# First and second layers of finished node tiles, placed by a table of trips instead of from trip 14 on

## The reference, cut to what matters

```python
# dst = sorted (6250 * u ** 2), u uniform; N_VERTEX rows are those of x
aggr = segment_sum(edge_attr, dst, num_segments=6250)          # 100,000 x 256 -> 6250 x 256
collected = concatenate([layernorm(x), aggr], axis=-1)         # 6250 x 512
h = relu(collected @ W1 + b1)                                  # first layer, 512 -> 256
h = relu(h @ W2 + b2)                                          # second layer
x = x + h @ W3 + b3                                            # third layer
x = x + ffn(layernorm(x))       # slice attention over all nodes, 8 heads of 64, then W_out
```

## Time and profile before

| | us |
|---|---|
| median of 3 runs (lowest, highest) | 680.67 (680.16, 681.75) |
| the profiled execution's own time | 680.57 |
| its span, first to last instruction | 678.8 |
| TensorE busy in the span | 603.0 (89%) |
| VectorE / ScalarE / GpSimd busy | 400.4 / 286.8 / 242.9 |
| moved by DMA | 133.88 MB, mean 197 GB/s |
| last turn of the edge part (L1243) starts | 324.17 |

### The profile page before, as it was taken

The page is one execution under the profiler, slowest core; times in us unless marked ns, Lnnn a source line. Parts: engine busy times, 40 slices in busy tenths (PEclk is TensorE's granted clock), DMA queues, the critical chain, the costliest instruction groups (busy, mean ns, idle before and its releaser), DMA issues.

```text
span 678.8 us, 12657 instructions
## 1 busy us (share of the span) xinstructions
PE 603.0 (89%) x3481; PEld 363.8 (54%) x3481; DVE 400.4 (59%) x1104; ACT 286.8 (42%) x422; POOL 242.9 (36%) x322
## 2 busy tenths in 40 slices
PE   5677777878798999899999889999999999799997
PEld 2355555545443444344689634444444443688886
DVE  6644444456454454444468888888888888522222
ACT  4244444545223223222210045555545454677773
POOL 3244444435000000000032366666666666344441
PEclk9799999989999999999999899999999999999999
DMA  8999999999999989994110123434343434122221
GB/s 305 339 403 406 405 403 407 392 385 383 386 378 328 329 289 321 314 323 148 31 43 3 32 47 62 77 62 77 62 77 62 76 63 77 16 78 77 77 77 69
DMA packets 107135, 133.88 MB, mean 197 GB/s; under 512 B 57595, under 2 KB 59601, under 8 KB 107109
## 3 DMA queue, kind: packets, MB, share of 16 engines
q1 hardware_dynamic: 106293, 133.29, 58.9%
q10 hardware_dynamic: 816, 0.26, 0.2%
HBM read 114.29 MB, written 6.40 MB: 178 GB/s over the span
## 4 chain that ended last, share of the span: by engine, by line
PE 59%; DMA 26%; DVE 7%; issue 4%; SPq 1%; DVEq 1%; POOL 1%; ACT 0%; POOLq 0%
DMA x_sb<-x_in 19%; PE ps L1520 12%; PE ps L1433 12%; PE ps L1450 11%; DMA ring_mem<-edge_attr_in 8%; PE ps L1249 6%; PE ps L1255 6%; PE ps L1212 4%; DVE big L933 2%; PE ps L1364 2%; PE ps L1426 2%; PE ps L1243 1%; DVE x_sb L1009 1%; DVE bn L1013 1%; DVEq L933 0%
## 5 line engine op out<-in xcount | busy, mean ns | idle before, releaser
L1212 PE MATMUL ps<-ring_mem,side 128*32 128x256 f32 (+1 forms) x1596 | 104.3, 395 | 44.6 <-DMA ring_mem<-edge_attr_in 44.6
L933 DVE TENSOR_TENSOR big<-big,ps 128x64 f32 x319 | 70.7, 222 | 109.5 <-PE ps L1243 72.1
L1212 PEld LDWEIGHTS ps<-ring_mem,side 128*32 128x32 f32 (+1 forms) x1596 | 51.0, 112 | 82.5 <-issue 46.1
L1433 PE MATMUL ps<-ring_mem,xn 128*128 128x512 f32 x196 | 93.3, 599 | 0.8 <-DVE ring_mem L1093 0.7
L1450 PE MATMUL ps<-side,ring_mem 128*128 128x512 f32 x196 | 92.3, 593 | 1.9 <-ACT ring_mem L740 1.9
L697 ACT ACTIVATE side<-ps 128x512 f32<-128x512 f32 (+1 forms) x50 | 25.6, 511 | 151.9 <-PE ps L1212 151.9
L629 POOL TENSOR_TENSOR ring_mem<-ring_mem 128x512 f32<-128x512 f32 x49 | 67.3, 1374 | 30.7 <-DVE ring_mem L1093 30.0
L1520 PE MATMUL ps<-side,ring_mem 128*128 128x256 f32 x360 | 77.9, 379 | 0.0
L1520 PEld LDWEIGHTS ps<-side,ring_mem 128*128 128x128 f32 x360 | 68.4, 190 | 9.3
L755 ACT ACTIVATE ring_mem<-ring_mem 128x512 f32<-128x512 f32 x49 | 30.9, 630 | 91.5 <-POOL ring_mem L622 91.5
L800 ACT ACTIVATE ring_mem<-big 128x1024 uint16 (+1 forms) x45 | 60.7, 1359 | 15.5 <-PE ps L1520 15.5
(11 more groups left out here) (136 smaller groups left out, 815.2 us busy)
## 6 DMA issues: line engine op xcount, KB each, us to landing
ring_mem<-edge_attr_in SPq DMA_DIRECT2D x84, 1024.0 KB, 8.5
ring_mem<-edge_attr_in SPq DMA_DIRECT2D x62, 256.0 KB, 4.3
x_sb<-x_in SPq DMA_DIRECT2D x24, 256.0 KB, 5.6
result<-ring_mem SPq DMA_DIRECT2D x24, 256.0 KB, 2.0
big<-side SPq DMA_TRANSPOSE x49, 3.0
side<-L_gnn_W_in SPq DMA_DIRECT2D x2, 256.0 KB, 10.1
ring_mem<-L_ffn_W_x_in SPq DMA_DIRECT2D x2, 256.0 KB, 2.8
ring_mem<-L_ffn_W_out_in SPq DMA_DIRECT2D x1, 512.0 KB, 3.9
```

The source lines that it names most:

```text
L933: dve.tensor_tensor(win, win, found[:, :, q * WINDOW:(q + 1) * WINDOW], ALU.add).then_inc(groups_added, 1)
L1212: return mm(ps[q * WINDOW:(q + 1) * WINDOW, SUM_BANKS[h], col:col + F], lhsT=hot[0:parts, h * 2 + j, t, :], rhs=ring8[0:parts, h * 2 + j, ...
L1433: last = mm(ps[:, 4 + k, :], lhsT=xn[:, r, k * P:(k + 1) * P], rhs=soft[:, r, :], start=isinstance(t, int) and t == 3, stop=isinstance(t, ...
```

## The change

The rule "first layer of tile i - 14, second of the tile before" becomes two tables of trips:

- the first layer's edge half runs in trips 10, 11, 13, 15, 16, 18, 19, 20, 22, 23, 24 (tiles 0 to 10), the second layer in trips 12, 14, 15, 17, 18, 20 to 24 (tiles 0 to 9). Where a trip has both, the second layer stands in front of the first, on TensorE, and `relu_two` in front of `relu_one` on ScalarE.
- in trips 10 to 13 they stand beside the work on x. `first_layer_x` writes both halves into bank 5 and counts once; the second layer uses banks 6 and 7 up to trip 13 and 4 and 5 after that.
- trips 10 to 24 are all written out; the loop over trips 2 to 9 stays.
- the weights of both layers are loaded in batch 3 instead of batch 26.
- the bounds `lowest` follow the table, by ten iotas on GpSimd instead of two.

```diff
@@ -43,9 +43,14 @@
 X_TRIPS = 13
-H1E_TRIP = 14
-H1E_TILES = 11
-H2_TILES = H1E_TILES - 1
+
+H1E_AT = {10: 0, 11: 1, 13: 2, 15: 3, 16: 4, 18: 5, 19: 6, 20: 7, 22: 8, 23: 9, 24: 10}
+H2_AT = {12: 0, 14: 1, 15: 2, 17: 3, 18: 4, 20: 5, 21: 6, 22: 7, 23: 8, 24: 9}
+H1E_TILES = len(H1E_AT)
+H2_TILES = len(H2_AT)
+TRIPS = 25
+
+H1E_RUNS = ((0, 10, 2), (2, 13, 1), (3, 15, 2), (5, 18, 3), (8, 22, 3))
 H2_CREDIT = 2
@@ -76,16 +81,8 @@
     trip(1, 2, P, "x")
     with eng.Fori(2, TWOS // UNROLL) as i:
         trip(i, 2, P, "x")
-    with eng.Fori(TWOS // UNROLL, X_TRIPS - 1) as i:
-        trip(i, 4, P, "x")
-    trip(X_TRIPS - 1, 4, P, "x")
-    trip(X_TRIPS, 4, P, "x")
-    trip(H1E_TRIP, 4, P, "h1")
-    with eng.Fori(H1E_TRIP + 1, FOURS // UNROLL) as i:
-        trip(i, 4, P, "h2")
-    with eng.Fori(FOURS // UNROLL, H1E_TRIP + H1E_TILES - 1) as i:
-        trip(i, 4, LAST_P, "h2")
-    trip(H1E_TRIP + H1E_TILES - 1, 4, LAST_P, "h2")
+    for i in range(TWOS // UNROLL, TRIPS):
+        trip(i, 4, P if i < FOURS // UNROLL else LAST_P, "x" if i <= X_TRIPS else "")
 def run_steps(eng, step, total, peel_front, loop_trips):
@@ -139,7 +136,7 @@
     assert F == KF * P and P == 2 * G and D == G and S == 512 and AGG >= N + WINDOW
     MLP_CHUNKS = (TILES - 1) // 4
     H1E_NODES = H1E_TILES * 4 * P
-    assert CHUNKS == UNROLL * (H1E_TRIP + H1E_TILES) and TAIL_GROUPS == 3 and (E - E_TAIL) % ROWS_PER_PART == 0
+    assert CHUNKS == UNROLL * TRIPS and TAIL_GROUPS == 3 and (E - E_TAIL) % ROWS_PER_PART == 0
     assert X_PAIRS == 2 * (X_TRIPS - 1) and H1E_TILES == MLP_CHUNKS - 1
     with ExitStack() as ctx:
@@ -368,6 +365,10 @@
         block = ctx.enter_context(nc.Block())
+        def h2_banks(i):
+
+            return [ps[:, (6 if i <= X_TRIPS else 4) + m, :] for m in range(KF)]
+
         def words(v):
             return v.bitcast(U16).rearrange("p (n h) -> p h n", h=2)
@@ -443,7 +444,7 @@
                     sp.dma_start(tiles_of(b * 2, 2).rearrange("p t f -> p (t f)"),
                                  x[bass.ds(b * (2 * P), 2 * P), :].rearrange("(p t) f -> p (t f)", p=P)
                                  ).then_inc(x_in, 16)
-                if isinstance(b, int) and b == X_PAIRS + 2:
+                if isinstance(b, int) and b == 3:
                     sp.dma_start(w1b_sb, w1[F:2 * F, :].rearrange("(k p) n -> p k n", p=P)).then_inc(w1b_in, 16)
                     sp.dma_start(w2_sb, w2.rearrange("(k p) n -> p k n", p=P)).then_inc(w2_in, 16)
@@ -552,8 +553,9 @@
             pool.wait_ge(rel_clear, 1)
             for a, first in enumerate((TWOS, FOURS)):
-                pool.iota(steps_of[:, a, :], [[UNROLL, H1E_TILES]], base=UNROLL * H1E_TRIP - first, channel_multiplier=-1,
-                          allow_small_or_imprecise_dtypes=True).then_inc(lowest_ready, 1)
+                for tile, at, n in H1E_RUNS:
+                    pool.iota(steps_of[:, a, tile:tile + n], [[UNROLL, n]], base=UNROLL * at - first, channel_multiplier=-1,
+                              allow_small_or_imprecise_dtypes=True).then_inc(lowest_ready, 1)
             pool.wait_ge(hot_ready, 1)
             pool.memset(big[:, CLEAR_A:KF * AGG], 0.0).then_inc(agg_clear, 1)
             pool.wait_ge(consts, 6)
@@ -673,9 +675,9 @@
                                ACT.Copy).then_inc(ln_t_ready, 1)
             def copy_h1x(i, n):
+                act.wait_ge(h1x_psum, i + 1)
                 for m in range(KF):
-                    act.wait_ge(h1x_psum, i * 2 + (m + 1))
-                    act.activation(h1x[:, m, bass.ds(i * 2 * P, n * P)], ps[:, 5 + m, 0:n * P],
+                    act.activation(h1x[:, m, bass.ds(i * 2 * P, n * P)], ps[:, 5, m * 2 * P:m * 2 * P + n * P],
                                    ACT.Identity, bias=b1_sb[:, m:m + 1]).then_inc(h1x_ready, 1)
             far_reg = []
@@ -704,10 +706,10 @@
                         norm_rows(b - 1, 2)
                     if isinstance(b, int) and b == X_PAIRS + 1:
                         norm_rows(X_PAIRS, 1)
-                elif h == 1:
-                    relu_one(i - H1E_TRIP, 4 * P)
-                    if what == "h2":
-                        relu_two(i - (H1E_TRIP + 1), 4 * P, [ps[:, 4 + m, :] for m in range(KF)])
+                if h == 1 and isinstance(i, int) and i in H2_AT:
+                    relu_two(H2_AT[i], 4 * P, h2_banks(i))
+                if h == 1 and isinstance(i, int) and i in H1E_AT:
+                    relu_one(H1E_AT[i], 4 * P)
                 if isinstance(b, int) and b == X_PAIRS + 3:
                     far_reg.append(act.value_load(far_i[0:1, 0:1], min_val=0, max_val=1))
@@ -852,10 +854,10 @@
             dve.tensor_scalar(row_ok[:, :], row_no[:, :], float(LAST_ROWS), None, ALU.is_lt).then_inc(groups_added, CREDIT)
             bases_one = into_bases(0, TWOS, 2, 7, 0)
-            dve.wait_ge(lowest_ready, 2)
+            dve.wait_ge(lowest_ready, 2 * len(H1E_RUNS))
             dve.tensor_scalar(steps_of, steps_of, 0.0, float(UNROLL * P), ALU.is_le, ALU.mult).then_inc(lowest_ready, 1)
             dve.memset(far_one[:, :], 0.0).then_inc(h2_ready, H2_CREDIT)
-            dve.wait_ge(lowest_ready, 3)
+            dve.wait_ge(lowest_ready, 2 * len(H1E_RUNS) + 1)
             dve.tensor_reduce(lowest[:, :], steps_of, AX.X, ALU.add).then_inc(h1e_added, 1)
             dve.wait_ge(h1e_added, 1)
             dve.wait_ge(dst_in, 16 * 5)
@@ -912,10 +914,9 @@
                     dve.wait_ge(win_psum, b * 2 + 2)
                     for j in range(2):
                         one_hot(b * 2 + (UNROLL + j), h * 2 + j)
-                if what != "x":
-                    if h == 0:
-                        dve.wait_ge(h1x_ready, 2 * (X_PAIRS + 1))
-                    add_h1e(i - H1E_TRIP, h)
+                if isinstance(i, int) and i in H1E_AT:
+                    dve.wait_ge(h1x_ready, 4 * (H1E_AT[i] + 1))
+                    add_h1e(H1E_AT[i], h)
                 if h == 0:
                     n_regs = UNROLL * groups
                     dve.load(base_regs[0:n_regs], base_i[0:1, bass.ds(sums_ahead(b * 2, groups), n_regs)])
@@ -1032,6 +1033,7 @@
                 folded[0] += 1
                 return folded[0]
+            dve.wait_ge(h1x_ready, 2 * (X_PAIRS + 1))
             for m in range(KF):
                 add_h1e(MLP_CHUNKS - 1, m)
             for m in range(KF):
@@ -1266,22 +1268,29 @@
                         first_layer_x(b - 3, 1 if isinstance(b, int) and b == X_PAIRS + 3 else 2)
                     if past(b, 2) and before(b, X_PAIRS + 3):
                         ln_transposes(b - 2, 1 if isinstance(b, int) and b == X_PAIRS + 2 else 2)
-                else:
-
+                if isinstance(i, int) and i in H2_AT:
+                    j = H2_AT[i]
+                    pe.wait_ge(w2_in, 16)
+                    pe.wait_ge(h1_ready, j + 1)
+                    if j == 0:
+                        pe.wait_ge(h1e_added, 2 * 2 + 1)
+                    elif j == 1:
+                        pe.wait_ge(h1x_ready, 2 * (X_PAIRS + 1))
+                    else:
+                        pe.wait_ge(h2_ready, H2_CREDIT + 2 * (j - 1) + h + 1)
+                    last = second_layer(j, h, h2_banks(i)[h], 4 * P)
+                    if h == KF - 1:
+                        last.then_inc(l2_psum, 1)
+                if isinstance(i, int) and i in H1E_AT:
+
+                    j = H1E_AT[i]
+                    pe.wait_ge(w1b_in, 16)
+                    pe.wait_ge(h1e_added, 2 * j + 1)
+                    if j == 2:
+                        pe.wait_ge(h2_ready, H2_CREDIT + 2)
                     if h == 0:
-                        pe.wait_ge(w1b_in, 16)
-                        pe.wait_ge(h1x_ready, 2 * (X_PAIRS + 1))
                         pe.wait_ge(groups_added, sums_ahead(b * 2, groups) + CREDIT)
-                    pe.wait_ge(h1e_added, (i - H1E_TRIP) * 2 + 1)
-                    first_layer_edges(i - H1E_TRIP, h).then_inc(h1e_psum, 1)
-                    if what == "h2":
-                        if h == 0:
-                            pe.wait_ge(w2_in, 16)
-                            pe.wait_ge(h1_ready, i - H1E_TRIP)
-                        pe.wait_ge(h2_ready, (i - H1E_TRIP) * 2 + (H2_CREDIT - 3 + h))
-                        last = second_layer(i - (H1E_TRIP + 1), h, ps[:, 4 + h, :], 4 * P)
-                        if h == KF - 1:
-                            last.then_inc(l2_psum, 1)
+                    first_layer_edges(j, h).then_inc(h1e_psum, 1)
                 turn(b, h, groups)
                 if isinstance(b, int) and b == 1:
                     rest_of_table()
@@ -1305,9 +1314,9 @@
                     pe.wait_ge(h1x_ready, i * 2)
                 for m in range(KF):
                     for k in range(KF):
-                        last = mm(ps[:, 5 + m, 0:n * P], lhsT=w1a_sb[:, k, m * P:(m + 1) * P],
+                        last = mm(ps[:, 5, m * 2 * P:m * 2 * P + n * P], lhsT=w1a_sb[:, k, m * P:(m + 1) * P],
```

(2 more changed lines are left out.)

## The result

The changed kernel takes 664.5 us in the median of four runs (661.8 to 665.7), the kernel before beside it 681.2. The ratio is 0.974, 95% interval 0.970 to 0.979. The profiled execution took 664.1 us with a span of 662.3, against 680.6 and 678.8: 16.5 us less. The forecast was 659.3 in a range of 654.5 to 668.5, so the range holds it, and of the 21.4 us that the sum promised 16.5 came.

What follows compares the result with a forecast made beforehand. TensorE was taken to bound trips 15 to 24, DMA those before. The last turn would move from 324.17 to 302.8 us, and 680.57 less 21.4 gave 659.2, forecast as 659.3 us, range 654.5 to 668.5.

Steps and rivals of the forecast that it cites:

- the sum: Running sum of trip ends from batch 19's turn to the last turn, which it put 21.4 us earlier.
- What bounds which stretch: Edge part of the kernel before: TensorE bounds trips 15 to 24, DMA those before.
- Trips 17 and 21 wait for edges: Sign of being right: DMA ends these trips, at 90.2 and 133.6 us, after TensorE's 88.5 and 132.0.
- The cover: Second layer in front hides TensorE's 1.41 us wait for VectorE's additions, 0.14 to spare; failing in part or whole: 8%.
- A trip ends at the later of TensorE's work and DMA's own pace: Rule for trips from 10 on: previous end plus TensorE's work, or DMA's 10.86 us a trip, whichever is later.
- Not lost: the ring of four chunks fills: Trips 10 to 13 put TensorE 3.7 us behind DMA; the chunk buffer fills meanwhile and trip 14 eats it.
- All that follows is the same program: After the last turn nothing changes, so every later step shifts by the same 21.4 us.
- relu_one's end for tiles 8 and 9: Trips 23 and 24: ends 2.29 us after the first layer, next second layer asks at 2.40; cost 0, at most 0.3 each.
- The weights: Loading both layers' 0.52 MB in batch 3 instead of 26 costs 1.37 us there, 0 if that stretch has a gap.
- DMA held its pace: Against the rival that DMA doesn't follow in trips 15 to 21, 12.3 us a trip, 669.3 us; chance 13%.
- code fetching: Rival: written-out trips must be fetched, some 10 blocks, 689 us at 3 us each; small 3%, large (slower) 3%.
- a second pass: Rival: a moved tile unfinished by its trip turns edges into "far" ones, costing hundreds of us; chance 1%.

Runs made afterwards that it cites:

- e7: The changed kernel with VectorE's load of the window bases ahead of add_h1e instead of behind it; median 666.91 us.
- e9: The changed kernel itself, run again as the measure for two kernels beside it; six runs from 663.3 to 666.9 us.
- e4: The change with the old table, no tile moved ahead, keeping second layer in front, written-out trips, one bank and early weights; 667.93 us, kernel before 684.04.
- e6: The change with only one of the two products in the first and second layers of trips 10 to 24, values wrong; 660.79 us.
- e8: The change with e5's turned batch, e7's early load, and second layers of tiles 5, 6 and 7 one trip sooner; median 663.17 us.
- e5: The change with, in the last odd batch, tile 10's first layer in front of tile 9's second layer again; median 663.81 us.
- e10: The change with both the turned last odd batch and VectorE's load ahead of add_h1e, same table; median 661.9 us.
- e3: The kernel before with trips 10 to 24 written out instead of in loops, nothing else; 680.11 us against 684.04, ratio 0.996.
- e2: The change with the old order inside a trip, first layer in front of the second, on TensorE and ScalarE; median 669.75 us.
- e1: The changed kernel itself, run again as the measure for three kernels beside it; median 663.82 us.

## Why the prediction was right, and where its sum was off

**What bounds which stretch: right.** TensorE's work by trip was met closely (trips 10 to 14: 58.7 against 58.6), and DMA's share went to full. Trips 17 and 21 wait for edges, but for 1.02 and 0.17 us where the sum had 1.7 and 1.6; the rest came as waits in the trips behind them.

**The cover: right, closer than it looked.** The additions no longer hold TensorE in trips with both layers. VectorE's chain got 1.1 us longer in even batches by the register load that lost its cover, which the sum had not listed; it stands in front of the window additions of the even batch, for which nobody waits until later, and taking it away (e7) moved the last turn by 0.4 us, no more than between two runs of the change (173.7 and, in e9, 173.3).

**"A trip ends at the later of TensorE's work and DMA's own pace": the step that failed, by 1.2 to 1.35 us in each of three trips.** The pace was read at turns of batches with other work behind the edges. From the second chunk's sums to the turn are 2.8 us in batch 43 (264.91 to 267.73) and 4.5 in batch 44 (270.30 to 274.84): with both layers the turn comes 1.7 us later after the same landing. Behind trips that DMA paces (14, 17, 21) the next trip took 13.1 to 13.2 us, not 11.86, and trip 15 of e4 13.04. Part of it, after trips 14 and 17, was taken back by the next slack; after trip 21 nothing follows that could.

**"Not lost: the ring of four chunks fills": mis-sized.** After the loaded trips 10 to 13 DMA ran at 367 GB/s instead of 386 from 160 to 200 us, 5% of 40 us = 2 us, and the mark after trip 17 came 1.5 later than the sum. The lag is the cause: e4, with no layers in those trips, has 385 GB/s in the same window, and e6, with half of their products, 386. e8 shows the same loss once more where TensorE fell some 4 us behind. A lag of 3.7 us (3.3 by the marks) is thus already beyond what the ring takes up. Of the 3.4 us by which the last turn missed the sum, this is 1.5; a DMA pace of 10.96 us a trip (trips 18 to 21, 43.9 us) instead of 10.86 is 0.4; trip 22 is 1.35.

**"All that follows is the same program": wrong by 1.7 us.** The prediction worked out relu_one's end for tiles 8 and 9 and forgot tile 10, whose second layer stands right behind the last turn, with no sums in between to hide ScalarE. e5 shows the cause, e10 the cost.

**The weights:** mark 19 came 1.15 us later in the first profile, 1.37 was counted. But with early weights it lay anywhere from 130.8 to 132.4, and without them at 131.05 and 131.64: their cost isn't told apart from the scatter of the start.

**Rivals.** DMA held its pace (384 and 386 GB/s from 200 to 280 us), code fetching was free (e3), and the time leaves no room for a second pass. The tables moved 14.3 us of TensorE's work (three first layers and one second), but the order carried three quarters of what the stretch gained (e4): the sum had this in it and the text didn't say it.

## What to carry to other kernels

When an engine is brought below the pace of the transfers, write the sum by batches and not by larger steps: the pace is that of landings, and what stands behind a landing in that batch comes on top. Before counting on a buffer to absorb uneven work, ask how late a slot may come free; here a ring of four chunks lost DMA time once TensorE was some 4 us behind. An order turned round moves a wait to whoever reads the thing that is now last, so look at the first reader behind the end of the section as well.

## What the runs showed of the hardware

- The same 3.00 us wait of TensorE was followed in some executions by the full clock and in others by a granted clock of 0.50, for up to 10 us; the six products behind it took 1.56 or 2.93 us. With the wait filled by 2.84 us of unused products the profiled run had the full clock there, and all five runs lay within 1.2 us.
- Shorter waits were followed by a lower clock too: behind a wait of 1.89 us (361.18 in the change) 16 products took 5.42 us, behind the same wait in e2 and e9 they took 3.73; behind one of 1.55 us in e1 the granted clock was 0.66 from 195 to 200 us.
- A consumer some 4 us behind the transfers cost them rate: 367 GB/s from 160 to 200 us against 385 and 386 in e4 and e6, and 329 in e8 from 260 to 270 us against 386 in the change.
- A load of window bases into VectorE's registers held its sequencer for 1.1 us each time; with another wait over it (e7, and the kernel before in all trips but one) it doesn't show.
- Code written out instead of looped (e3) took 13.13 us a trip against 13.30. Its page counts 18 blocks of q8, 0.29 MB, where the kernel before has 13, and no wait of VectorE's sequencer came with them.
